# A two-layer cross-attention on one core: loads on two queues, a reordered front, and the statistics and normals of the main loop moved behind the maximum

## The chip, the cores and the metric

The kernel runs on one core of one Trainium2 chip. The metric is the device time in microseconds (us) of one execution. The core has five engines that matter here, each with its own instruction stream in program order: TensorE (PE, matrix multiplications and transposes), VectorE (DVE), ScalarE (ACT), GpSimd (POOL) and SyncE (SP, which here only issues loads and stores). They meet only through counted semaphores: an instruction waits until a count is reached, and all that stands behind it on its engine waits with it.

## The reference

The input is 32 batches of 256 tokens by 256 features, `x` and `ctx`. Layer 0 is a 16-head attention whose result for batch 0 alone (`att[0]`) is added to every batch. Layer 1 normalises both sides, attends over the normalised context, passes the result through a hidden layer of 4, attends over that once more, and adds it up.

```
q, k, v = heads(tgt @ Wq.T), heads(memory @ Wk.T), heads(memory @ Wv.T)
att = softmax(q k^T / sqrt(16)) v
x = tgt + att[0]                                # layer 0

norm_X, norm_F_L = LN(ctx, w1, b1), LN(x, w2, b2)
attended = softmax(norm_F_L norm_X^T / 16) norm_X
h = gelu(attended @ fc1_w.T + fc1_b)
cross = h @ fc2_w.T + fc2_b
norm_cross = LN(cross, w3, b3)
self = softmax(norm_cross norm_cross^T / 16) norm_cross
out = norm_F_L + gamma2 * (cross + gamma1 * self)
```

## The kernel before

Every engine's program is written out by hand, and nothing reorders it: what stands first in the code is issued first. The work falls into four stages.

The **front** (to about 14 us) loads the parameters, the transposed batch 0 of both inputs and the three weights, all on SP's queue, and then the first 8 batches (`SLOTS`) of `ctx` and `x` into `cN` and `xN`. PE first multiplies a constant by itself (`keep_busy`), then makes Q (into `qT`), K and the parameter products (`operand_products`), and the two halves of V (`value_projection`). VectorE prepares small operands one after the other (`link`: each waits for the one ahead of it), among them the output operand `stR` (`output_operand`, lines 336 to 347), and masks K into `kTm`.

The **head loop** (to about 37 us) does batch 0's 16 heads in 8 pairs `p`: scores, maxima, exponentials, transposes, products with V. Beside it VectorE takes the statistics of the context's first six batches and at `p == 6` their variances; GpSimd takes one root for all three pairs of batches and normalises them.

Then comes the **change of stage** (to about 55 us): `tgt2` (that is `att[0]`) is made and added to the first batches, and the `x` side of the first batches is normalised.

The **main loop** has 32 slots, one per batch `b`, and each engine has its own loop over them. Batches go in pairs: pair `k` holds batches `2k` and `2k+1`. In slot `b` PE does, in this order: `turned(k+1, m)` with `m = b % 2` (line 897: in an even slot it transposes the context side of the next pair, in an odd slot the `x` side of the next pair; it waits for the normalised halves of both batches of the pair), `score(b)` (line 960), one or two small products that depend on `b % 4`, and `weights_turned(b-1)` (line 968). ACT empties the transposes out of the PSUM banks, and makes the exponentials. The scores of a pair use transposes of the slots ahead.

A batch's way to `turned` goes over three engines. GpSimd adds `tgt2` to the `x` side (`add`, line 621). VectorE takes statistics of both sides (`statistics`, line 369), and of each pair the negative mean and the variance (`variances`, lines 377 and 380). GpSimd takes the inverse root (`root`, line 628, which also waits for the variances) and normalises the context side (line 641); VectorE normalises the `x` side (`normal`, line 389). VectorE also takes the maximum of the scores (`maximum(b)`, line 512), which waits for `score(b)`.

GpSimd's slot `b` is `add(b+6)`, then in an even slot `root(k+2)`, then the context side's `normal(b+4)`. VectorE's slot, the lines that the change moves:

```
if k + 3 < PAIRS:
    statistics(b + 6, 0)
    statistics(b + 6, 1)
    if m == 1:
        variances(k + 3)
maximum(b)
...
if k + 2 < PAIRS:
    normal(b + 4)
```

In the slots 20 to 29 VectorE has the first half of the algebra on the hidden layer as well (`LATE`). The **tail** (from about 168 us) does the second attention over `cross` and stores the output.

## Time and profile before

| | |
|---|---|
| timed runs | 245.39, 248.79 and 255.70 us, median 248.79 |
| profiled execution | 244.72 us, of which the span from first to last instruction is 242.9 |
| busy share of the span | PE 88%, DVE 79%, ACT 62%, POOL 51% |
| chain that ended last | PE 55%, DVE 27%, issue 8%, ACT 6%, POOL 1% |
| mean granted clock of PE | 0.967 of full speed |

The busy shares are means over stages with different limits, so they do not say which engine bounds a stage. The chain of waits, followed back from the last instruction, passes over VectorE, PE and ACT in turn up to 55 us, runs on PE alone from 59 to 117 us, is mixed with VectorE up to 147 us, and is on PE again up to 164 us.

### The profile page before, as it was taken

How to read it: one execution, taken by the hardware profiler on the slowest of the kernel's cores; microseconds unless marked ns; L12 is line 12 of the kernel's file. 1: busy time of each engine (PE TensorE's matmuls, PEld its weight loads, DVE VectorE, ACT ScalarE, POOL GpSimd, SP SyncE). 2: the span in 40 equal slices, each digit the busy share in tenths (PEclk: the TensorE clock that was granted, in tenths of full speed). 3: DMA queues.
4: the chain of work that ended last, by engine and by line, in shares of the span. 5: the costliest groups of instructions: out<-in, count | busy, mean ns of one | idle time of the engine just before them, and what ended most of it. 6: DMA issues, size and time to landing. Idle time of an engine off the chain costs nothing.

```text
span 242.9 us, 4973 instructions
## 1 busy us (share of the span) xinstructions
PE 212.8 (88%) x1758; PEld 154.1 (63%) x1758; DVE 193.1 (79%) x376; ACT 151.3 (62%) x292; POOL 124.4 (51%) x184
## 2 busy tenths in 40 slices
PE   6989989677999999999999899999978569999850
PEld 6766647445878789687796777967646234444420
DVE  7888858899999987798799999933557966777773
ACT  2167866216778678676796977856695435676520
POOL 6000096776999999969788948400002621221340
PEclk9999999999999999999999999999999857999995
DMA  6990000253454415554154000000000022443468
GB/s 183 381 346 3 1 4 0 81 155 111 174 173 136 164 53 173 175 153 159 51 174 158 3 1 3 0 1 3 0 3 1 0 89 86 172 168 149 174 229 326
DMA packets 14713, 26.82 MB, mean 110 GB/s; under 512 B 1760, under 2 KB 1760, under 8 KB 14688
## 3 DMA queue, kind: packets, MB, share of 16 engines
q1 hardware_dynamic: 14688, 26.50, 31.4%
q8 instruction: 14, 0.23, 0.4%
q14 instruction: 11, 0.09, 0.1%
HBM read 18.11 MB, written 8.39 MB: 109 GB/s over the span
## 4 chain that ended last, share of the span: by engine, by line
PE 55%; DVE 27%; issue 8%; ACT 6%; POOL 1%; DVEq 0%; ACTq 0%; POOLq 0%
PE psum L960 15%; PE psum L897 7%; DVE bn L369 6%; DVE xN L389 5%; PE psum L968 5%; PE psum L852 5%; DVE nm L552 3%; PE psum L1074 3%; PE psum L998 2%; PE psum L910 2%; PE psum L980 2%; PE psum L925 2%; PE psum L938 2%; DVE nmax L512 2%; DVE Fall L567 1%
## 5 line engine op out<-in xcount | busy, mean ns | idle before, releaser
L960 PE MATMUL psum<-XT,Fall 128*128 128x256 f32 x256 | 60.9, 381 | 1.8 <-ACT Fall L742 1.8
L960 PEld LDWEIGHTS psum<-XT,Fall 128*128 128x128 f32 x256 | 46.1, 190 | 7.2 <-ACT Fall L742 2.2
L641 POOL TENSOR_SCALAR cN<-cN,nmean,rstd 128x256 f32<-128x256 f32 x64 | 38.5, 612 | 2.4 <-POOL rstd L628 2.3
L621 POOL TENSOR_TENSOR xN<-xN,tgt 128x512 f32<-128x512 f32 x28 | 35.7, 1277 | 1.6 <-DVE xN L389 1.6
L389 DVE TENSOR_SCALAR xN<-xN,bn,rstd 128x256 f32<-128x256 f32 x64 | 34.1, 576 | 0.7 <-POOL rstd L628 0.7
L765 ACT ACTIVATE PT<-psum 128x512 f32<-128x512 f32 x32 | 19.1, 598 | 24.3 <-PE psum L968 24.2
L772 ACT ACTIVATE E<-psum,nmax 128x256 f32<-128x256 f32 x64 | 26.7, 474 | 11.0 <-DVE nmax L512 10.9
L628 POOL TENSOR_TENSOR rstd<-vps,minus_half 128x8 f32<-128x8 f32 (+1 forms) x16 | 25.0, 1564 | 15.7 <-DVE vps L380 15.6
L685 POOL CAST sC<-co 128x160 bf16<-128x160 f32 x8 | 2.6, 321 | 59.3 <-DVE co L561 59.3
L512 DVE TENSOR_REDUCE nmax<-psum 128x2 f32<-128x512 f32 x32 | 21.9, 685 | 13.8 <-PE psum L960 13.3
L567 DVE TENSOR_TENSOR Fall<-psum,Fall 128x1024 f32<-128x1024 f32 x15 | 18.1, 1219 | 10.1 <-PE psum L1107 10.1
L739 ACT ACTIVATE XT<-psum,b1s,w1s 128x512 f32<-128x512 f32 x32 | 23.1, 792 | 3.7 <-PE psum L897 3.7
L742 ACT ACTIVATE Fall<-psum,par 128x512 f32<-128x512 f32 x32 | 23.4, 796 | 3.2 <-PE psum L897 3.2
L852 PE MATMUL psum<-ident 128*128 128x128 f32 x144 | 23.3, 307 | 1.9 <-POOL ident L593 1.9
L852 PEld LDWEIGHTS psum<-ident 128*128 128x128 f32 x144 | 19.4, 208 | 5.5 <-issue 3.6
L369 DVE BATCH_NORM_STATS2 bn<-cN 128x6 f32<-128x512 f32 x32 | 22.3, 696 | 0.4 <-DVE r L445 0.2
L552 DVE TENSOR_REDUCE nm<-psum 128x4 bf16<-128x1024 f32 x16 | 19.5, 1218 | 3.4 <-PE psum L1042 3.3
L369 DVE BATCH_NORM_STATS2 bn<-xN 128x6 f32<-128x512 f32 x32 | 21.8, 687 | 0.0
L968 PE MATMUL psum<-ident,E 128*128 128x128 f32 x128 | 20.2, 280 | 0.3 <-ACT E L772 0.2
L968 PEld LDWEIGHTS psum<-ident,E 128*128 128x128 f32 x128 | 14.3, 141 | 8.3 <-issue 6.3
L897 PE MATMUL psum<-ident,xN 128*128 128x128 f32 x128 | 17.1, 274 | 2.6 <-DVE xN L389 2.3
L897 PE MATMUL psum<-ident,cN 128*128 128x128 f32 x128 | 16.9, 274 | 0.1
(157 smaller groups left out, 346.0 us busy)
## 6 DMA issues: line engine op xcount, KB each, us to landing
cN<-ctx SPq DMA_DIRECT2D x32, 256.0 KB, 2.9
xN<-x SPq DMA_DIRECT2D x32, 256.0 KB, 3.8
out<-Fall SPq DMA_DIRECT2D x32, 256.0 KB, 2.3
x0T<-x0t SPq DMA_DIRECT2D x1, 256.0 KB, 2.7
wqT<-wqt SPq DMA_DIRECT2D x1, 256.0 KB, 2.9
c0T<-c0t SPq DMA_DIRECT2D x1, 256.0 KB, 4.0
wkT<-wkt SPq DMA_DIRECT2D x1, 256.0 KB, 4.3
wvT<-wvt SPq DMA_DIRECT2D x1, 256.0 KB, 4.5
```

The lines of the kernel that those rows point to most:

```text
L369: dve.bn_stats(bn[:, (b // 2) % 4, side, b % 2, :], src[:, b % SLOTS, :].rearrange("p (t d) -> p d t", t=NT)).then_inc(st_ok, 1)
L389: dve.tensor_scalar(own, own, stat(p, 1, m, t, 1), root_of(p, 1, m, t), ALU.subtract, ALU.mult)\
L512: dve.tensor_reduce(nmax[:, b % 2, :], tiles(bank[SBANK1[b % 3]]), AX.X, ALU.max, negate=True)\
L552: dve.tensor_reduce(nm2[:, p % 2, :, 0:NT], scored(p).rearrange("p (m t k) -> p m t k", m=2, t=NT), AX.X, ALU.max, negate=True).then_inc(m ...
L621: pool.tensor_tensor(xN[:, b % SLOTS, :], xN[:, b % SLOTS, :], tgt2[:, :, :].rearrange("p t d -> p (t d)"), ALU.add).then_inc(y_ok, 1)
L628: pool.tensor_tensor(rstd[:, p % 4, sides, :].rearrange("p s k -> p (s k)"), vps[:, p % 4, sides, :].rearrange("p s k -> p (s k)"), minus_ ...
L641: pool.tensor_scalar(own, own, nmean[:, p % 4, NT * m + t:NT * m + t + 1], root_of(p, 0, m, t), ALU.add, ALU.mult)\
L772: act.activation(E[:, b % 2, t * N:(t + 1) * N], bank[SBANK1[b % 3]][:, t * N:(t + 1) * N], ACT.Exp, bias=nmax[:, b % 2, t:t + 1]).then_in ...
L852: pe.matmul(bank[b][:, 0:P], ident[:, :], ident[:, :], start=True, stop=True)
L897: last = pe.transpose(bank[TBANK[n % 3]][:, m * N + t * P:m * N + (t + 1) * P], z[:, (2 * p + m) % SLOTS, t * D + c * P:t * D + (c + 1) * ...
L960: last = pe.matmul(bank[SBANK1[b % 3]][:, t * N:(t + 1) * N], Fall[:, b, c, t * P:(t + 1) * P], XT[:, p % 4, c, m * N:(m + 1) * N], start= ...
L968: last = pe.transpose(bank[SBANK1[b % 3]][:, k * N + t * P:k * N + (t + 1) * P], E[:, b % 2, t * N + k * P:t * N + (k + 1) * P], ident[:, :])
```

## The change

It reorders the front and the main loop, and computes the same.

- **Loads.** `x0T` and `c0T` are issued by ACT's queue and the three weights by SP's, side by side. Behind them SP loads eight batches of `ctx` first and then eight of `x`.
- **Front on PE.** `keep_busy` multiplies `meanw`, which is GpSimd's first memset, eight times in place of seven. K is made and masked in two halves. The first half of V comes behind the first head scores and the second in the head loop's pass 2, and ACT copies them out in passes 1 and 3. `operand_products`, the first `project` and `project_back` move to the change of stage.
- **Output operand** on GpSimd, 17 small steps, each behind the one ahead.
- **Roots by pair.** The variances of the first three pairs are taken in the head loop's passes 1, 3 and 5, and GpSimd roots and normalises one pair at a time.
- **GpSimd's `add(5)`** waits until VectorE has normalised the first four batches of `x`.
- **Main loop on VectorE.** In slot `b` the maximum now comes first, then the statistics of batch `b+5` (in place of `b+6`), in an even slot the variances of the pair of `b+5`, and last the normal of batch `b+3` (in place of `b+4`). PE's, ACT's and GpSimd's slots keep their order.

```diff
-        for dst, src, arrived in ((x0T, x0t, q_in), (wqT, wqt, q_in), (c0T, c0t, k_in), (wkT, wkt, k_in),
-                                  (wvT, wvt, v_in)):
-            sp.dma_start(dst[:, :, :], src).then_inc(arrived, 16)
-
-        for p in range(PAIRS):
-            if p >= SLOTS // 2:
-                sp.wait_ge(t_mm, turns_to(p - SLOTS // 2, 1))
+        sp.dma_start(wqT[:, :, :], wqt).then_inc(q_in, 16)
+        sp.dma_start(wkT[:, :, :], wkt).then_inc(k_in, 16)
+        sp.dma_start(wvT[:, :, :], wvt).then_inc(v_in, 16)
+
+        for src, dst, arrived in ((c_d, cN, c_in), (x_d, xN, x_in)):
+            for b in range(SLOTS):
+                sp.dma_start(dst[:, b, :], src[b, :, :]).then_inc(arrived[b], 16)
+        for p in range(SLOTS // 2, PAIRS):
+            sp.wait_ge(t_mm, turns_to(p - SLOTS // 2, 1))
...
-        def output_operand(part):
-
-            if part == 0:
...
-        output_operand(0)
-        dve.wait_ge(k_mm, 1)
-        for e, m in enumerate(("even", "odd")):
-            dve.tensor_scalar(kTm[:, e, :, :], tiles(bank[1]), c_(m), None, ALU.mult).then_inc(kT_ok, 1)
-        dve.wait_ge(qk_mm, 1)
-        link(dve.tensor_copy(Q[:, :], bank[5][:, 0:(H + 1) ** 2]))
-        link(dve.tensor_copy(K[:, :], bank[5][:, 64:64 + U * U]), "QK")
-        output_operand(1)
+        def masked(o):
+            dve.wait_ge(k_mm, o + 1)
+            for e, m in enumerate(("even", "odd")):
+                dve.tensor_scalar(kTm[:, e, o, :], bank[(1, 5)[o]][:, 0:N], c_(m), None, ALU.mult).then_inc(kT_ok, 1)
+
+        masked(0)
...
+        def first_variances(p):
+            dve.wait_ge(st_ok, 2 * p + 2)
+            dve.tensor_scalar(nmean[:, p, :].rearrange("p (m t) -> p m t", t=NT),
+                              bn[:, p, 0, :, :].rearrange("p m (t k) -> p m t k", t=NT)[:, :, :, 1],
+                              -1.0, None, ALU.mult).then_inc(vps_first, 1)
+            dve.tensor_scalar(vps[:, p, 0, :].rearrange("p (m t) -> p m t", t=NT),
+                              bn[:, p, 0, :, :].rearrange("p m (t k) -> p m t k", t=NT)[:, :, :, 2],
+                              1.0 / D, EPS, ALU.mult, ALU.add).then_inc(vps_first, 1)
...
+                if p == 0:
+                    masked(1)
                 if p < 2 * EARLY:
                     statistics(p, 0)
-                elif p == 2 * EARLY:
-                    dve.wait_ge(st_ok, 2 * EARLY)
-                    dve.tensor_scalar(nmean[:, 0:EARLY, :].rearrange("p q (m t) -> p q m t", t=NT),
-                                      bn[:, 0:EARLY, 0, :, :].rearrange("p q m (t k) -> p q m t k", t=NT)[:, :, :, :, 1],
-                                      -1.0, None, ALU.mult).then_inc(vps_first, 1)
-                    dve.tensor_scalar(vps[:, 0:EARLY, 0, :].rearrange("p q (m t) -> p q m t", t=NT),
-                                      bn[:, 0:EARLY, 0, :, :].rearrange("p q m (t k) -> p q m t k", t=NT)[:, :, :, :, 2],
-                                      1.0 / D, EPS, ALU.mult, ALU.add).then_inc(vps_first, 1)
+                if p in (1, 3, 5):
+                    first_variances(p // 2)
...
         add(3)
+        dve.wait_ge(qk_mm, 1)
+        link(dve.tensor_copy(Q[:, :], bank[7][:, 0:(H + 1) ** 2]))
+        link(dve.tensor_copy(K[:, :], bank[7][:, 64:64 + U * U]), "QK")
         normal(0)
         normal(1)
         statistics(2, 1)
...
         statistics(4, 1)
         normal(2)
         normal(3)
-        statistics(5, 1)
-        variances(2)
...
         for b in range(B):
             k, m, q = b // 2, b % 2, b // 4
-            if k + 3 < PAIRS:
-                statistics(b + 6, 0)
-                statistics(b + 6, 1)
-                if m == 1:
-                    variances(k + 3)
             maximum(b)
             if b % 4 == 2:
                 values(q)
             if b % 4 == 3 and q >= 1:
                 saved(q - 1)
-            if k + 2 < PAIRS:
-                normal(b + 4)
-            if b == 18:
-                output_operand(2)
+            if b == 0:
+                statistics(2 * EARLY - 1, 1)
+                variances(EARLY - 1)
+            elif b + 5 < B:
+                statistics(b + 5, 0)
+                statistics(b + 5, 1)
+                if m == 0:
+                    variances((b + 5) // 2)
+            if 4 <= b + 3 < B:
+                normal(b + 3)
             for part in LATE.get(b, ()):
                 algebra(0, part)
...
+        pool.memset(meanw[:, :], 1.0 / D).then_inc(consts, 1)
...
+        oc = [0]
+
+        def step(ins):
+            ins.then_inc(operand_ok, 1)
+            oc[0] += 1
+            pool.wait_ge(operand_ok, oc[0])
...
+        pool.wait_ge(alg, ALG["prods"])
+        step(pool.tensor_tensor(g12[:, :], c_("g1"), c_("g2"), ALU.mult))
+        for c in range(DC):
+            step(pool.tensor_scalar(Rt[:, c, 0:H], a5[:, c, 0:H], c_("g2", c), None, ALU.mult))
+            step(pool.tensor_scalar(Rt[:, c, H:CO], MT[:, c, :], g12[:, c:c + 1], None, ALU.mult))
+            step(pool.tensor_scalar(Rcut[:, c, 0:1], a5[:, c, H:H + 1], c_("g2", c), None, ALU.mult))
+            step(pool.tensor_tensor(Rt[:, c, CO - 1:CO], Rt[:, c, CO - 1:CO], Rcut[:, c, 0:1], ALU.add))
+        for part in range(2):
+            to = stR[:, :, part, :]
+            step(pool.tensor_copy(slots(to, CO, SLOTS_L[0]), repeated(Rt[:, :, :], 3)))
+            step(pool.tensor_tensor(Rcut[:, :, :], Rt[:, :, :], to[:, :, 0:CO], ALU.subtract))
+            step(pool.tensor_copy(slots(to, CO, SLOTS_L[1]), repeated(Rcut[:, :, :], 2)))
+            step(pool.tensor_tensor(to[:, :, 5 * CO:6 * CO], Rcut[:, :, :], to[:, :, 3 * CO:4 * CO], ALU.subtract))
+        ALG["stR"] = oc[0]
...
+            if b == 5:
+                pool.wait_ge(zy_ok, 8)
...
-        pool.wait_ge(vps_first, 2)
-        pool.tensor_tensor(rstd[:, 0:EARLY, 0, :], vps[:, 0:EARLY, 0, :],
-                           minus_half[:, 0:EARLY * 2 * NT].rearrange("p (q k) -> p q k", q=EARLY), ALU.pow)\
-            .then_inc(root_first, 1)
-        for b in range(2 * EARLY):
-            normal(b)
+        for p in range(EARLY):
+            pool.wait_ge(vps_first, 2 * p + 2)
+            pool.tensor_tensor(rstd[:, p, 0, :], vps[:, p, 0, :], minus_half[:, 0:2 * NT], ALU.pow).then_inc(root_first, 1)
+            normal(2 * p)
+            normal(2 * p + 1)
...
+        act.dma_start(x0T[:, :, :], x0t).then_inc(q_in, 16)
+        act.dma_start(c0T[:, :, :], c0t).then_inc(k_in, 16)
...
+            if p in (1, 3):
+                values_copied(p // 2)
...
+        turned_values(0)
...
-            if b % 4 == 1:
+            if b % 4 == 1 and q >= 1:
...
-                pe.matmul(bank[b][:, 0:P], ident[:, :], ident[:, :], start=True, stop=True)
-
-        pe.wait_ge(consts, 4)
-        keep_busy(7, 4)
+                pe.matmul(bank[b][:, 0:P], meanw[:, :], meanw[:, :], start=True, stop=True)
+
+        pe.wait_ge(consts, 1)
+        keep_busy(8, 4)
...
+        pe.wait_ge(k_in, 32)
+        for o in range(2):
+            for c in range(DC):
+                last = pe.matmul(bank[(1, 5)[o]][:, 0:N], wkT[:, c, o * P:(o + 1) * P], c0T[:, c, :],
+                                 start=c == 0, stop=c == DC - 1)
+            last.then_inc(k_mm, 1)
...
-        operand_products()
-        pe.wait_ge(v_in, 16)
-        value_projection(0)
...
-                if p == 1:
-                    pe.wait_ge(v1_ok, 2)
...
+                pe.wait_ge(v_in, 16)
+                value_projection(0)
+            if p == 2:
                 value_projection(1)
             if 1 <= p <= NHP:
                 if p == 1:
-                    pe.wait_ge(alg, ALG["QK"])
+                    pe.wait_ge(kT_ok, 4)
...
-        keep_busy(11, 7)
...
+        project(0)
+        operand_products()
+        keep_busy(3, 0)
+        project_back(0)
+        keep_busy(4, 0)
...
-            if b % 4 == 1 and q < QUADS:
+            if b % 4 == 1 and 1 <= q < QUADS:
                 project(q)
             if b % 4 == 2:
-                project_back(q)
+                if q >= 1:
+                    project_back(q)
```

VectorE in the main loop, slot 2 and the first of slot 3, before: `nmax` is the maximum, `V1` the values' copy of slot 2, `xN` the normals, `BN_STATS` the statistics.

```order
L369 BN_STATS bn<-cN 128x6
L369 BN_STATS bn<-xN 128x6
L512 TENSOR_REDUCE nmax<-psum 128x2
L523 COPY V1<-psum 128x8x4
L389 TENSOR_SCALAR xN<-xN,bn,rstd 128x256 x2
L369 BN_STATS bn<-cN 128x6
L369 BN_STATS bn<-xN 128x6
L377 TENSOR_SCALAR nmean<-bn 128x4
L380 TENSOR_SCALAR vps<-bn 128x8
L512 TENSOR_REDUCE nmax<-psum 128x2
```

And now:

```order
L505 TENSOR_REDUCE nmax<-psum 128x2
L516 COPY V1<-psum 128x8x4
L356 BN_STATS bn<-cN 128x6
L356 BN_STATS bn<-xN 128x6
L364 TENSOR_SCALAR nmean<-bn 128x4
L367 TENSOR_SCALAR vps<-bn 128x8
L376 TENSOR_SCALAR xN<-xN,bn,rstd 128x256 x2
L505 TENSOR_REDUCE nmax<-psum 128x2
```

The normals stood right behind a slot's maximum, and the statistics and variances between them and the next maximum; now statistics and variances follow the maximum and the normals come last.

VectorE ahead of the main loop's first maximum, before, from the normals of batches 2 and 3:

```order
L389 TENSOR_SCALAR xN<-xN,bn,rstd 128x256 x4
L369 BN_STATS bn<-xN 128x6
L380 TENSOR_SCALAR vps<-bn 128x4
L369 BN_STATS bn<-cN 128x6
L369 BN_STATS bn<-xN 128x6
L512 TENSOR_REDUCE nmax<-psum 128x2
L389 TENSOR_SCALAR xN<-xN,bn,rstd 128x256 x2
```

And now, from the same normals to the second maximum:

```order
L376 TENSOR_SCALAR xN<-xN,bn,rstd 128x256 x4
L505 TENSOR_REDUCE nmax<-psum 128x2
L356 BN_STATS bn<-xN 128x6
L367 TENSOR_SCALAR vps<-bn 128x4
L505 TENSOR_REDUCE nmax<-psum 128x2
L356 BN_STATS bn<-cN 128x6
L356 BN_STATS bn<-xN 128x6
L376 TENSOR_SCALAR xN<-xN,bn,rstd 128x256 x2
```

Between the normals and the first maximum stood four instructions, of which three are statistics; now the maximum follows the normals at once.

## Rows read from the trace of the kernel before

**Rows 1.** The windows view: length, busy us of PE, PEld, DVE, ACT, POOL, clock, DMA.

```profile
5.40:15.00 9.60, 8.99 (x52) 6.99 (x52) 7.66 (x28) 2.70 (x7) 0.00 (x0) 1.00 1.03 383
37.40:59.40 22.00, 16.56 (x116) 12.52 (x115) 20.79 (x42) 9.34 (x16) 14.67 (x16) 1.00 0.30 96
59.40:117.00 57.60, 57.56 (x442) 47.22 (x441) 50.74 (x103) 44.06 (x87) 53.20 (x58) 1.00 0.44 147
189.00:195.00 6.00, 2.85 (x30) 1.54 (x29) 5.86 (x8) 2.60 (x5) 4.18 (x8) 0.82 0.00 0
195.00:200.00 5.00, 3.18 (x24) 1.63 (x26) 3.41 (x6) 1.83 (x3) 1.46 (x4) 0.50 0.29 108
```

**Rows 2.** The timeline of PE, four slots: start, length, instruction.

```profile
93.26 1.89 PE L960 MATMUL psum<-XT,Fall 128*128 128x256 f32 x8
...
96.30 1.89 PE L960 MATMUL psum<-XT,Fall 128*128 128x256 f32 x8
...
100.47 1.89 PE L960 MATMUL psum<-XT,Fall 128*128 128x256 f32 x8
...
103.98 1.04 PE L897 MATMUL psum<-ident,xN 128*128 128x128 f32 x8
104.85 1.89 PE L960 MATMUL psum<-XT,Fall 128*128 128x256 f32 x8
...
108.11 1.89 PE L960 MATMUL psum<-XT,Fall 128*128 128x256 f32 x8
```

**Rows 3.** The timeline of VectorE in slots 14 and 15.

```profile
102.40 0.69 DVE L512 TENSOR_REDUCE nmax<-psum 128x2 f32<-128x512 f32 x1 [1.61 <-PE psum L960]
103.00 0.18 DVE L523 COPY V<-psum 128x32 f32<-128x32 f32 x1
...
104.78 0.69 DVE L369 BATCH_NORM_STATS2 bn<-cN 128x6 f32<-128x512 f32 x1
...
106.11 0.17 DVE L377 TENSOR_SCALAR nmean<-bn 128x4 f32<-128x4 f32 x1
106.19 0.16 DVE L380 TENSOR_SCALAR vps<-bn 128x8 f32<-128x8 f32 x1
```

**Rows 4.** The timeline of all engines: one root, two normals on each side.

```profile
77.23 0.16 DVE L380 TENSOR_SCALAR vps<-bn 128x8 f32<-128x8 f32 x1
...
77.47 1.65 POOL L628 TENSOR_TENSOR rstd<-vps,minus_half 128x8 f32<-128x8 f32 x1 [0.18 <-DVE vps L380]
...
78.01 0.72 DVE L389 TENSOR_SCALAR xN<-xN,bn,rstd 128x256 f32<-128x256 f32 x2
...
79.29 1.09 POOL L641 TENSOR_SCALAR cN<-cN,nmean,rstd 128x256 f32<-128x256 f32 x2 [0.18 <-POOL rstd L628]
80.34 1.27 POOL L621 TENSOR_TENSOR xN<-xN,tgt 128x512 f32<-128x512 f32 x1
81.60 1.29 POOL L641 TENSOR_SCALAR cN<-cN,nmean,rstd 128x256 f32<-128x256 f32 x2
```

**Rows 5.** The timeline of VectorE ahead of and at the loop's start.

```profile
43.55 1.38 DVE L389 TENSOR_SCALAR xN<-xN,bn,rstd 128x256 f32<-128x256 f32 x4 [0.31 <-POOL rstd L628]
...
47.54 3.27 DVE L389 TENSOR_SCALAR xN<-xN,bn,rstd 128x256 f32<-128x256 f32 x4 [0.43 <-POOL rstd L628]
...
52.75 0.67 DVE L512 TENSOR_REDUCE nmax<-psum 128x2 f32<-128x512 f32 x1
```

**Rows 6.** The timeline of PE: scores of slot 2 and of slot 28.

```profile
55.69 1.99 PE L960 MATMUL psum<-XT,Fall 128*128 128x256 f32 x8 [0.66 <-ACT Fall L742]
...
154.30 1.89 PE L960 MATMUL psum<-XT,Fall 128*128 128x256 f32 x8
```

**Rows 7.** The chain of waits, head of the program: start, length, line.

```profile
1.90 3.36 PE psum L852 x14
...
9.16 0.81 PE psum L874 x8
...
13.71 1.16 PE psum L910 x8
```

More of the change, by code:

```diff
@@ L53 @@
 QUADS = B // 4
+EARLY = 3
 SLOT = 64
@@ L634, in normal @@
             if p < EARLY:
[L635 removed]
+                pool.wait_ge(root_first, p + 1)
             else:
@@ L861, in _ @@
         last.then_inc(mean_mm, 1)
-        for arrived, n, w, src, b, done in ((q_in, 32, wqT, x0T, 0, q_mm), (k_in, 32, wkT, c0T, 1, k_mm)):
-            pe.wait_ge(arrived, n)
-            for o in range(2):
-                for c in range(DC):
-                    last = pe.matmul(bank[b][:, o * N:(o + 1) * N], w[:, c, o * P:(o + 1) * P], src[:, c, :],
-                                     start=c == 0, stop=c == DC - 1)
-            last.then_inc(done, 1)
+        pe.wait_ge(q_in, 32)
+        for o in range(2):
+            for c in range(DC):
+                last = pe.matmul(bank[0][:, o * N:(o + 1) * N], wqT[:, c, o * P:(o + 1) * P], x0T[:, c, :],
+                                 start=c == 0, stop=c == DC - 1)
+        last.then_inc(q_mm, 1)
+        pe.wait_ge(k_in, 32)
+        for o in range(2):
+            for c in range(DC):
+                last = pe.matmul(bank[(1, 5)[o]][:, 0:N], wkT[:, c, o * P:(o + 1) * P], c0T[:, c, :],
+                                 start=c == 0, stop=c == DC - 1)
+            last.then_inc(k_mm, 1)
         def operand_products():
```

36 lines of the change are left out of this document (15 added, 21 removed).

## The prediction

> **What bounds the kernel now.** I read the chain of waits first, for where it stays on one engine: from 59 to 117 us it is PE alone. The windows view confirms it: PE is busy for 57.56 of 57.60 us there, GpSimd for 53.20, VectorE for 50.74 [rows 1]. So whatever makes PE wait in the main loop adds to the time one for one, while work taken from VectorE gives nothing. Ahead of the loop it is otherwise: from 37.4 to 59.4 PE is busy for 16.56 of 22.00 us and VectorE for 20.79, so there VectorE's order is what counts.
>
> The timeline of PE shows what the loop costs [rows 2]. Slot 12's scores start at 93.26, slot 13's at 96.30, slot 14's at 100.47, slot 15's at 104.85, slot 16's at 108.11: 14.85 us for four slots, without a gap. The transposes ahead of a score take 0.87 (103.98 to 104.85).
>
> **The main loop, step by step.** Let e be an even slot. In slot e+1 PE transposes the x side of batches e+2 and e+3. Before, the normal of batch e+3 stood on VectorE right behind the maximum of slot e-1, so it was done before PE wanted it. Now it stands in slot e, behind that slot's maximum, two statistics and the variances, and this maximum waits for score(e). PE's program is in order, so score(e+1) stands behind transposes that wait for a result of score(e): a loop over two engines where there was none.
>
> Its length, from the start of score(e): the maximum starts 1.93 later (100.47 to 102.40) and holds VectorE for 0.60; where slot e is the third of four, the values' copy adds 0.10 [rows 2, 3]. The two statistics up to the negative mean take 1.33, the mean 0.08, the variance 0.16 [rows 3], the two normals 0.72, as where they ran beside a root [rows 4]. That is 4.82, or 4.92. Two of the pair's eight transposes do not need batch e+3; the other six take 0.65. So score(e+1) starts 5.47 or 5.57 after score(e), where it took 3.04 (slot 12 to 13) and 4.38 (slot 14 to 15): PE's small work between fills only part of the wait.
>
> A second loop goes over GpSimd. The variances of the pair of batches e+4 and e+5 are now taken in slot e behind the maximum, where they used to be taken ahead of the maximum of slot e-1. GpSimd then does the root, a normal, an add and a normal, and PE's slot e+2 transposes these batches. From score(e): 1.93 + 0.60 + 1.33 + 0.08 as above; 0.24 to the root, 1.82 to the first normal, 1.05 to the add, 1.26 to the second normal, and 1.29 of that [rows 4]; 0.65 of transposes. That is 10.25, and 10.35 with the values' copy. PE's own way, with the first loop, is 5.47 + 4.17 = 9.64, or 5.57 + 3.26 = 8.83 [rows 2]. The longer sets the pair: about 10.3 where two slots now take 7.43. Both loops close anew in every pair, so slack ahead of the loop does not help.
>
> Thirteen pairs lie between the scores of slot 2 and of slot 28: six at 10.25, six at 10.35, and the last without its add (10.35 - 1.26 = 9.09), 132.7 us. Before it was 154.30 - 55.69 = 98.6 [rows 6]. That is **+34.1**. Slot 29 waits for one more normal, without statistics: 1.93 + 0.60 + 0.72 + 0.65 = 3.90 in place of 3.04, **+0.9**. VectorE's algebra in the slots from 20 on now lies behind the normals and beside PE's transposes and scores; it costs nothing as long as it fits into the wait that the second loop leaves VectorE. Its eight operand steps, now on GpSimd, lay beside a busy PE: nothing. On GpSimd the 17 steps lie where it did nothing at all (0.00 us busy from 5.4 to 15 us [rows 1]) and ahead of a first root that needs them no earlier; cover gone, each would cost a fraction of a us once.
>
> **The change of stage and the front.** Four normals took 3.27 beside GpSimd's adds and 1.38 alone [rows 5]; `add(5)` now waits for them, which gives 1.89. The first maximum came at 52.75, 1.94 behind the end of those normals, and now follows at once. Together 3.83 for the first exponentials, and with them for the evacuation and score(2) behind them on ACT. But the adds that waited now run beside the normals of batch 4, half as many: about 0.95 back, and 0.15 for the copies of the parameter products. I take 2.7. Bounds: 1.5, if the late adds hold up the slots' statistics as well, and 3.8.
>
> In the head the parameter products' 0.81 leave PE's path, and the second head score no longer waits for V (it started at 13.71) [rows 7]. K's halves let the first score start before the second half is masked. That is worth up to 2.4 at the second score; V's second half in pass 2, on PE about as long as a head score's 1.16, the copies on ACT and the small variances on VectorE take part of it back. I take 1.3, bounds 0 and 2.4. PE's warm-up starts earlier, behind the first memset, but has eight products in place of seven, and 3.36/7 = 0.48 of that is lost again [rows 7]; this is inside the bounds. Front in all **-4.0** (-1.5 to -6.2).
>
> Of the two load queues I expect nothing that can be seen: PE is busy for 8.99 of 9.60 us from 5.4 to 15, so at most 0.6 is waited for there, and the DMA engines are full (share 1.03) [rows 1]. The Trainium skill (Trainium Kernel Development and Optimization, Key Constraints) says that DMAs from SP's and ACT's queues run on the same 16 engines, and that several issuers save issue time alone. The full share agrees; by the rule the term is zero, against it 0.6 at most.
>
> Sum: 242.9 + 34.1 + 0.9 - 4.0 = 273.9 of span. Around the span lie 244.72 - 242.9 = 1.8: 275.7 against the profiled execution. The median of the timed runs lies 4.1 above that execution and the lowest 0.7; I add 2.3, between them: **278.0**.
>
> **Rivals.**
>
> *GpSimd is not the longer loop (0.11).* If its normals come without the add between them mattering, only the first loop holds: 6 x 9.64 + 7 x 8.83 = 119.7, +21.0 in place of +34.1, and 265. For it: GpSimd has more free time in a slower loop; against it: root, normal, add and normal are in order, and the lengths above are those of single instructions.
>
> *PE's clock falls (0.12).* In the first loop PE would stand still for some 2.4 us once in four slots (4.82, less the 3.04 - 0.87 of score and weights and the 0.22 of the first two transposes [rows 2]). The clock was at full speed where PE was busy for 75% (37.4 to 59.4), and fell to half after a stretch with 2.85 of 6.00 busy [rows 1]; the new loop has 7.43 of 10.3, 72%. At half speed the second loop grows by a score and the transposes, 1.89 + 0.65, to 12.8, and PE's own way, 9.24 on average, by 1.89 + 0.65 + 3.7 to 15.5. If it is half for half of the time, 13 pairs take 13 x 12.9 = 168: 35 us more, 313.
>
> *The shift is absorbed (0.08).* The other side: if normal(e+3) is ready within 2.17 + 0.22 = 2.4 us of score(e)'s start, where PE's own work ends, PE sees no wait, and the front's gain stands alone: 242.9 - 4.0 + 1.8 + 2.3 = 243. The rows give 4.82, so VectorE's part would have to take less than half of its time. I leave it a chance only for an error in my reading of who waits for whom: 0.04 faster, 0.04 within 2%.
>
> *Root and normals exclude each other (0.03).* If the normals could not start before the root ends (0.24 + 1.65 behind the variance's start instead of 0.16), score(e+1) would start 1.7 later, pairs take 11.4 and 10.6, and 13 of them 142: 287. But two normals took 0.72 in the middle of a root of 1.65 [rows 4]. The Trainium skill (SBUF, Who interferes with whom) says that VectorE's `tensor_scalar` in its two-port mode and any GpSimd instruction hold one shared pair of ports in turn, and that the later one waits for the whole of the other. The 3.27 beside the adds agrees with it; the 0.72 beside the root does not, and that is the neighbour that the normals of even slots will have.
>
> **How the numbers follow.** The forecast is the likeliest case, 278 (0.66). Its own spread: instructions beside GpSimd's that come 0.5 later in each pair (+6.5), a front that gives 1.5 (+2.5), the median's place (-1.6 to +1.8), and a clock that falls now and then. The range goes from 262, below the first rival, to 296; it leaves out the clock at half for long and the absorbed shift, 0.20 together. A change within 2% is about what cannot be told from none here. Slower by over 2%: all but the absorbed case, 0.92.
>
> **What would show it.** In the changed kernel's main loop PE has gaps in every pair: one ahead of the x side's transposes, released by VectorE's normals, and one ahead of the context side's, released by GpSimd's. VectorE's maximum starts at once behind the score, and VectorE and GpSimd stand idle in every pair too. Score 2 starts near 51.7, and score 28 some 133 us later. The first maximum follows its normals at once. I am wrong if PE stays busy without gaps from 59 to 117, if the gaps are there but only VectorE ends them, or if the granted clock in the loop is below 1.

## The result and the profile after

The changed kernel takes **278.23 us** (median of 4 runs, 275.83 to 278.85) against 250.51 for the kernel before (4 runs, 245.39 to 255.7). The ratio is 1.124, with an interval of 1.107 to 1.142: slower. The profiled execution took 278.69 us, 276.9 of it span. Ratios leave out executions in which a lower granted clock had lengthened the whole run.

The windows view of the changed kernel first. Its columns are the window, its length, then the busy us of PE, PEld, DVE, ACT and POOL, the granted clock, the DMA share and GB/s.

```profile
5.40:15.00 9.60, 9.29 (x54) 6.84 (x54) 6.97 (x20) 3.53 (x9) 4.21 (x17) 1.00 1.04 389
...
59.00:117.00 58.00, 45.94 (x321) 35.74 (x323) 33.97 (x70) 31.56 (x61) 35.63 (x40) 0.96 0.35 109
117.00:185.00 68.00, 52.09 (x392) 39.95 (x384) 48.20 (x108) 40.49 (x75) 40.76 (x46) 1.00 0.20 63
```

In the main loop PE is busy for 45.94 of 58.00 us, where it had been for 57.56 of 57.60 [rows 1]. No engine is full: VectorE has 33.97 and GpSimd 35.63. A loop in which all engines wait is bound by a chain that goes from one to the next. The waits view of the loop from 72 to 182 us names its links (sum in us, times, longest):

```profile
POOL rstd L648 <- DVE vps L367: 43.8, 11, 5.1
DVE nmax L505 <- PE psum L993: 36.8, 20, 4.4
...
PE psum L930 <- DVE xN L376: 17.5, 11, 2.3
...
PE psum L930 <- POOL cN L661: 8.3, 10, 1.3
```

GpSimd waits for the variances, VectorE for the scores, and PE once in a pair for VectorE's normals and once for GpSimd's. One pair of it, in the timeline of all engines (start, length, engine, line, instruction; the wait ahead of it in brackets):

```profile
104.55 1.89 PE L993 MATMUL psum<-XT,Fall 128*128 128x256 f32 x8
...
106.48 0.69 DVE L505 TENSOR_REDUCE nmax<-psum 128x2 f32<-128x512 f32 x1 [0.99 <-PE psum L993]
...
107.09 0.69 DVE L356 BATCH_NORM_STATS2 bn<-cN 128x6 f32<-128x512 f32 x1
...
108.49 0.16 DVE L367 TENSOR_SCALAR vps<-bn 128x8 f32<-128x8 f32 x1
108.56 0.73 DVE L376 TENSOR_SCALAR xN<-xN,bn,rstd 128x256 f32<-128x256 f32 x2
108.73 1.74 POOL L648 TENSOR_TENSOR rstd<-vps,minus_half 128x8 f32<-128x8 f32 x1 [3.71 <-DVE vps L367]
109.35 0.87 PE L930 MATMUL psum<-ident,xN 128*128 128x128 f32 x6 [2.25 <-DVE xN L376]
...
110.06 1.89 PE L993 MATMUL psum<-XT,Fall 128*128 128x256 f32 x8
...
110.65 1.09 POOL L661 TENSOR_SCALAR cN<-cN,nmean,rstd 128x256 f32<-128x256 f32 x2 [0.18 <-POOL rstd L648]
...
111.70 1.27 POOL L641 TENSOR_TENSOR xN<-xN,tgt 128x512 f32<-128x512 f32 x1
...
112.96 1.09 POOL L661 TENSOR_SCALAR cN<-cN,nmean,rstd 128x256 f32<-128x256 f32 x2
...
113.81 1.68 DVE L376 TENSOR_SCALAR xN<-xN,bn,rstd 128x256 f32<-128x256 f32 x2
...
114.10 0.87 PE L930 MATMUL psum<-ident,cN 128*128 128x128 f32 x6 [0.37 <-POOL cN L661]
...
114.81 1.89 PE L993 MATMUL psum<-XT,Fall 128*128 128x256 f32 x8
```

Read down it goes round once: score of slot 12, maximum 1.93 later, two statistics, the variance, the root, GpSimd's normal, add and normal, the transposes, and the score of slot 14. 104.55 to 114.81 is 10.26 us, where slots 12 and 13 had needed 7.21 (93.26 to 100.47 [rows 2]). The x side's loop closes inside it: 104.55 to 110.06, 5.51.

PE's timeline at the loop's start answers to [rows 6], VectorE's to [rows 5]. PE:

```profile
50.48 1.99 PE L993 MATMUL psum<-XT,Fall 128*128 128x256 f32 x8
...
58.01 3.02 PE L993 MATMUL psum<-XT,Fall 128*128 128x256 f32 x8
...
62.20 1.89 PE L993 MATMUL psum<-XT,Fall 128*128 128x256 f32 x8
...
67.00 1.49 PE L930 MATMUL psum<-ident,xN 128*128 128x128 f32 x6 [2.25 <-DVE xN L376]
68.28 3.00 PE L993 MATMUL psum<-XT,Fall 128*128 128x256 f32 x8
...
186.01 1.89 PE L993 MATMUL psum<-XT,Fall 128*128 128x256 f32 x8
```

VectorE:

```profile
46.07 1.38 DVE L376 TENSOR_SCALAR xN<-xN,bn,rstd 128x256 f32<-128x256 f32 x4 [0.43 <-POOL rstd L648]
47.53 0.69 DVE L505 TENSOR_REDUCE nmax<-psum 128x2 f32<-128x512 f32 x1
...
51.97 1.91 DVE L376 TENSOR_SCALAR xN<-xN,bn,rstd 128x256 f32<-128x256 f32 x2
53.80 0.68 DVE L505 TENSOR_REDUCE nmax<-psum 128x2 f32<-128x512 f32 x1
```

Score 2 starts at 50.48 (before 55.69), score 28 at 186.01 (before 154.30): the 13 pairs take 135.53 in place of 98.61. Two scores, of slots 3 and 5, take 3.02 and 3.00 in place of 1.89, at a clock that had fallen (0.59 of full speed from 57.0 to 61.0 and from 67.0 to 71.2). From score 31 (197.30) to the end it is 79.6; before, 164.55 to 242.9, 78.4.

### The profile page after: what moved, and what is told of

Read it like the earlier page. It is cut to its first block and busy times, and to the rows that moved or that the text cites. A ratio compares the mean times of both kernels' runs of the same rounds, so it can differ in the third digit from the quotient of the medians.

```text
span 276.9 us, 4969 instructions
## 1 busy us (share of the span) xinstructions
PE 222.0 (80%) x1752; PEld 157.3 (57%) x1752; DVE 185.9 (67%) x367; ACT 153.2 (55%) x292; POOL 125.6 (45%) x203
## 5 line engine op out<-in xcount | busy, mean ns | idle before, releaser
L993 PE MATMUL psum<-XT,Fall 128*128 128x256 f32 x256 | 63.1, 391 | 1.1 <-ACT Fall L767 1.1
L648 POOL TENSOR_TENSOR rstd<-vps,minus_half 128x8 f32<-128x8 f32 (+1 forms) x16 | 26.1, 1628 | 60.4 <-DVE vps L367 60.1
L993 PEld LDWEIGHTS psum<-XT,Fall 128*128 128x128 f32 x256 | 47.9, 198 | 7.1 <-ACT Fall L767 1.5
L930 PE MATMUL psum<-ident,xN 128*128 128x128 f32 x128 | 21.0, 292 | 24.0 <-DVE xN L376 24.0
L661 POOL TENSOR_SCALAR cN<-cN,nmean,rstd 128x256 f32<-128x256 f32 x64 | 34.8, 554 | 2.6 <-POOL rstd L648 2.3
L376 DVE TENSOR_SCALAR xN<-xN,bn,rstd 128x256 f32<-128x256 f32 x64 | 34.1, 578 | 0.5 <-POOL rstd L648 0.4
L930 PEld LDWEIGHTS psum<-ident,xN 128*128 128x128 f32 x128 | 15.1, 147 | 27.7 <-DVE xN L376 26.2
L930 PE MATMUL psum<-ident,cN 128*128 128x128 f32 x128 | 19.3, 279 | 8.3 <-POOL cN L661 8.3
L878 PE MATMUL psum<-meanw 128*128 128x128 f32 x138 | 23.3, 314 | 1.0 <-POOL meanw L583 1.0
L878 PEld LDWEIGHTS psum<-meanw 128*128 128x128 f32 x138 | 19.2, 212 | 4.6 <-issue 3.6
L930 PEld LDWEIGHTS psum<-ident,cN 128*128 128x128 f32 x128 | 14.1, 141 | 11.7 <-POOL cN L661 10.9
```

The lines of the kernel that those rows point to most:

```text
L376: dve.tensor_scalar(own, own, stat(p, 1, m, t, 1), root_of(p, 1, m, t), ALU.subtract, ALU.mult)\
L648: pool.tensor_tensor(rstd[:, p % 4, sides, :].rearrange("p s k -> p (s k)"), vps[:, p % 4, sides, :].rearrange("p s k -> p (s k)"), minus_ ...
L661: pool.tensor_scalar(own, own, nmean[:, p % 4, NT * m + t:NT * m + t + 1], root_of(p, 0, m, t), ALU.add, ALU.mult)\
L878: pe.matmul(bank[b][:, 0:P], meanw[:, :], meanw[:, :], start=True, stop=True)
L930: last = pe.transpose(bank[TBANK[n % 3]][:, m * N + t * P:m * N + (t + 1) * P], z[:, (2 * p + m) % SLOTS, t * D + c * P:t * D + (c + 1) * ...
L993: last = pe.matmul(bank[SBANK1[b % 3]][:, t * N:(t + 1) * N], Fall[:, b, c, t * P:(t + 1) * P], XT[:, p % 4, c, m * N:(m + 1) * N], start= ...
```

## The experiments

The places that every run below is read by, from its profiled execution: the start of score 2, the 13 pairs from there to score 28, and what lies between score 31 and the end of the span. The median is of all timed runs; the ratio leaves out the same executions as above.

| kernel | span | clock | score 2 | 13 pairs | after score 31 | median | ratio (interval) |
|---|---|---|---|---|---|---|---|
| before | 242.9 | 0.967 | 55.69 | 98.6 | 78.4 | 246.3 to 250.5 | |
| after | 276.9 | 0.954 | 50.48 | 135.5 | 79.6 | 278.23 | 1.124 (1.107 to 1.142) |
| e1_slots_back | 243.2 | 0.949 | 54.62 | 98.5 | 79.9 | 244.20 | 0.997 (0.994 to 0.9996) |
| e2_slots_only | 280.5 | 0.945 | 55.83 | 135.3 | 78.1 | 281.74 | 1.146 (1.138 to 1.154) |
| e3_normals_first | 295.1 | 0.923 | 49.99 | 154.1 | 79.8 | 298.66 | 1.215 (1.203 to 1.226) |
| e4_variances_early | 277.2 | 0.920 | 49.82 | 138.1 | 77.9 | 279.08 | 1.136 (1.131 to 1.142) |
| e6_first_max | 245.7 | 0.944 | 50.79 | 103.1 | 81.6 | 249.56 | 1.004 (0.9997 to 1.008) |
| e5_first_max_busy | 249.0 | 0.923 | 50.49 | 103.0 | 85.2 | 251.24 | 1.021 (1.014 to 1.028) |
| e7_adds_together | 280.4 | 0.913 | 50.77 | 138.5 | 79.8 | 282.15, one run | |
| e8_busy_3_5 | 275.5 | 0.957 | 50.63 | 135.6 | 78.0 | 277.32, one run | |
| e9_adds_busy | 279.8 | 0.906 | 50.37 | 128.7 | 88.9 | 281.62 and 269.88 | |
| e10_after_busy | 277.2 | 0.955 | 50.88 | 134.7 | 79.8 | 279.52 | 1.136 (1.127 to 1.145) |
| e11_tail_busy | 239.9 | 0.973 | 53.94 | 99.7 | 76.1 | 242.35 | 0.986 (0.981 to 0.992) |
| e12_before_tail | 242.6 | 0.979 | 56.40 | 98.6 | 77.4 | 244.13 | 0.995 (0.992 to 0.998) |

**Which part of the change costs the time?** e1 takes VectorE's main loop back and keeps the rest; e2 makes that edit alone in the kernel before.

```diff
 e1, against the changed kernel (e2 is the same edit the other way, in the kernel before)
+        statistics(5, 1)
+        variances(2)
         for b in range(B):
+            if k + 3 < PAIRS:
+                statistics(b + 6, 0)
+                statistics(b + 6, 1)
+                if m == 1:
+                    variances(k + 3)
             maximum(b)
...
-            if b == 0:
-                statistics(2 * EARLY - 1, 1)
-                variances(EARLY - 1)
-            elif b + 5 < B:
-                statistics(b + 5, 0)
-                statistics(b + 5, 1)
-                if m == 0:
-                    variances((b + 5) // 2)
-            if 4 <= b + 3 < B:
-                normal(b + 3)
+            if k + 2 < PAIRS:
+                normal(b + 4)
```

> The changed kernel with VectorE's main loop alone put back: statistics of batch b+6 and the variances ahead of maximum(b), normal(b+4) behind it, and statistics(5, 1) and variances(2) ahead of the loop. Theory (the two loops through score, maximum and normals make all of the loss): PE has no gaps from slot 4 on, the scores of slot 2 and slot 28 lie 98 to 100 us apart again instead of 135.5 (186.01 - 50.48), and the front keeps most of its gain, so the span is 239 to 242 against 276.9 now and 242.9 before. Rival (the front is what slows: operand steps on GpSimd, the add(5) that waits for zy_ok 8, loads in another order): most of the loss stays, a span over 265.

> The kernel before with VectorE's main loop of the changed one, nothing else. Theory: the whole loss comes back, the scores of slot 2 and slot 28 lie 132 to 137 us apart, pairs take 10.25 and 10.35, and without the front's gain of head and add(5) the span is 277 to 281. Rival (the front is part of the loss): a span under 265.

The two runs split the change in two without a rest. With the slots put back the pairs take 98.5 again, with the slots alone 135.3. The whole loss lies in the order of VectorE's slot. What e1 does not keep is most of the front's gain: score 2 comes 1.1 earlier than before, not 4 to 5, and 0.3% is left of it at the end. That part of its expectation missed: the span is 243.2, not 239 to 242.

**Is it the loop that was named?** e3 and e4 each shift one link of the chain, so that the two theories of its length part.

```diff
 e3, against the changed kernel
             if b % 4 == 3 and q >= 1:
                 saved(q - 1)
+            if 4 <= b + 3 < B:
+                normal(b + 3)
...
-            if 4 <= b + 3 < B:
-                normal(b + 3)
```

> The changed kernel, with normal(b+3) right behind the slot's maximum and the statistics and variances behind it. This shortens the loop over VectorE from 5.47 to 1.93 + 0.60 + 0.72 + 0.65 = 3.90 and lengthens the way to the variances by the two normals, 0.65 to 0.72. Theory (the longer loop over GpSimd sets the pair, 10.26 and 10.36 in the trace): pairs get LONGER, to 10.9 to 11.1, and 13 pairs take 8 to 9 us more than the changed kernel's; the gap ahead of the x side's transposes nearly goes (to under 1 us) and the one ahead of the context side's grows by about 2. Rival (VectorE's late normals are what costs, GpSimd is slack that follows): pairs fall to 7.9 to 8.1, 13 pairs to some 103, the span to about 246.

With VectorE's normals ahead of the statistics PE's first pause should shrink, and the way to the root should grow. It did both. The timeline of all engines of e3, over the end of one pair and the next:

```profile
90.36 0.88 PE L930 MATMUL psum<-ident,xN 128*128 128x128 f32 x6 [0.53 <-DVE xN L376]
...
97.28 0.87 PE L930 MATMUL psum<-ident,cN 128*128 128x128 f32 x6 [1.80 <-POOL cN L661]
```

VectorE's normals now end only 0.53 of PE's pauses here, and GpSimd's 1.80. Pairs without a fallen clock took 10.95 to 10.98 (63.66 to 74.62, 74.62 to 85.60, 108.97 to 119.92), as the loop over GpSimd said; had VectorE's normals been the bound, they would have come down. Thirteen such pairs would be 142.5, near the 143.5 to 144.5 expected. The other 11.6 of the 154.1 lie in the first pair (13.67) and in pairs with a score at a fallen clock: those of slots 8, 14, 18 and 26 took 3.33 to 3.52 (granted clock 0.54 from 85.6 to 89.0). No run held the clock in e3.

```diff
 e4, against the changed kernel
-            elif b + 5 < B:
-                statistics(b + 5, 0)
-                statistics(b + 5, 1)
-                if m == 0:
-                    variances((b + 5) // 2)
+            if b + 6 < B:
+                statistics(b + 6, 0)
+                statistics(b + 6, 1)
+                if m == 1:
+                    variances((b + 6) // 2)
```

> The changed kernel, with the statistics one batch further ahead (b+6) behind the maximum, and the variances of a pair in the odd slot ahead, as early as in the kernel before; normal(b+3) stays last. This takes the loop over GpSimd away and leaves the one over VectorE without variances: 1.93 + 0.60 + 1.24 + 0.72 + 0.65 = 5.14, 5.24 with the values' copy. Theory: no gap that GpSimd ends; pairs take 5.14 + 4.17 = 9.31 and 5.24 + 3.26 = 8.50, 13 pairs 115 us, the span about 256 to 259. Rival (the normals' place alone is the loss, so nothing is won): 13 pairs stay at 130 or more.

The variances move into the odd slot, so the root is early. The loop over GpSimd opens indeed: no pause of PE in the loop is ended by GpSimd any more, and the pairs that begin in the third of four slots take 8.76 (95.76 to 104.52; 8.50 expected). But those that begin in the first of four take 12.06 (83.70 to 95.76; 9.31 expected). The timeline there:

```profile
87.44 1.70 DVE L376 TENSOR_SCALAR xN<-xN,bn,rstd 128x256 f32<-128x256 f32 x2
87.70 1.29 POOL L641 TENSOR_TENSOR xN<-xN,tgt 128x512 f32<-128x512 f32 x1
...
89.20 1.23 PE L930 MATMUL psum<-ident,xN 128*128 128x128 f32 x6 [2.96 <-DVE xN L376]
...
90.22 3.26 PE L993 MATMUL psum<-XT,Fall 128*128 128x256 f32 x8
```

The early root has pushed GpSimd's add beside VectorE's normals, which now take 1.70 in place of 0.73. PE's pause grows to 2.96, the clock falls (0.59 from 89.2 to 93.4), and the score takes 3.26. The expectation missed: one loop went, the other grew by 1.0, and the clock fell behind the longer pause. Of the 2.75 over the 9.31 expected, the normals are 0.97, the slower transposes 0.36 (1.23 against 0.87) and the slower score 1.37. That the clock would have stood without the longer pause was not tried in e4. e7 tries the same from GpSimd's side, with both adds in the even slot, ahead of the root, so that nothing stands between its two normals.

```diff
 e7, against the changed kernel (GpSimd's slot)
-            if k + 3 < PAIRS:
+            if m == 0 and k + 3 < PAIRS:
                 add(b + 6)
+                add(b + 7)
```

> The changed kernel, with GpSimd's adds of both batches of a pair in the even slot, ahead of the root, so that no add lies between the two normals of a pair. Theory: the loop over GpSimd shrinks by 1.26, to 8.99 and 9.09, and the other loop takes over where it is longer: pairs of 9.64 (even slot the first of four) and 9.09 (third of four), 13 pairs 121 to 125 us instead of 135.5, the span near 265; the gap that GpSimd ends goes in the first kind of pair. Rival (GpSimd does not set the pair): no change of the distance of the scores.

Again GpSimd ends no pause, and again only every other pair is short: 9.15 (96.76 to 105.91; 9.09 expected), then 11.46 (105.91 to 117.37) in place of 9.64. PE's timeline in e7:

```profile
105.91 1.89 PE L994 MATMUL psum<-XT,Fall 128*128 128x256 f32 x8
...
110.86 0.88 PE L931 MATMUL psum<-ident,xN 128*128 128x128 f32 x6 [2.23 <-DVE xN L376]
111.58 3.19 PE L994 MATMUL psum<-XT,Fall 128*128 128x256 f32 x8
```

The pause is 2.23, no longer than the 2.25 of the changed kernel at 109.35, and score to score is 5.67 against its 5.51; but here the score takes 3.19 (granted clock 0.64 from 111.0 to 114.7), there 1.89. That asked for a run in which only the clock differs. e9 is e7 with seven filler products of TensorE in every fourth slot, which take up part of the pause; e10 is the changed kernel with the same filler.

```diff
 e9, against e7; e10, against the changed kernel (PE's slot)
+            if b % 4 == 1 and q >= 1 and k + 1 < PAIRS:
+                pe.wait_ge(V1_ok, q)
+                keep_busy(7, 6)
```

> e7 (both adds in one slot) with seven filler products of TensorE at the start of every fourth slot, behind the wait for the weighted values. Two theories of why e7's shorter pairs gave no shorter loop. If it was the granted clock, which fell to half at each of e7's scores behind the two adds (2.94 to 3.62 us in place of 1.89), the filler holds it: scores near 1.89, pairs of 9.64 and 9.15 in turn, some 122 us for the 13 pairs and a span near 265. If the pairs are long because VectorE's chain is long there and the clock only follows it, the scores shorten and the pause ahead of them grows by as much: pairs of 11.5 and 9.15 as in e7, a span of 279 to 281, or a little more for the filler itself.

The filler held the clock. The windows view from 72 to 188 us, of e9:

```profile
72.00:188.00 116.00, 104.27 (x803) 83.34 (x795) 83.09 (x177) 72.31 (x137) 71.23 (x82) 1.00 0.25 81
```

and of e7:

```profile
72.00:188.00 116.00, 97.44 (x663) 72.15 (x662) 72.47 (x165) 66.14 (x125) 68.36 (x78) 0.92 0.25 82
```

PE's timeline of e9, over one such pair:

```profile
102.04 1.89 PE L994 MATMUL psum<-XT,Fall 128*128 128x256 f32 x8
...
107.01 0.87 PE L931 MATMUL psum<-ident,xN 128*128 128x128 f32 x6 [0.85 <-DVE xN L376]
107.72 1.89 PE L994 MATMUL psum<-XT,Fall 128*128 128x256 f32 x8
...
111.88 1.89 PE L994 MATMUL psum<-XT,Fall 128*128 128x256 f32 x8
```

Score to score is 5.68 as in e7, so VectorE's chain is as long as it was, and the filler lay wholly in the pause. But the score takes 1.89, and the pair 9.84 (102.04 to 111.88) in place of 11.46, the other still 9.15. From slot 4 to slot 28 every score of e9 takes 1.89. The first theory holds for these pairs: it was the clock that ate e7's gain. The 13 pairs come to 128.7, not 122, mostly since slots 2 to 4 took 13.87: the filler starts with slot 5, and slot 3's score took 3.62. Behind the loop the granted clock was 0.80 from 190 to 240, and the last part took 88.9, so the span of 279.8 says little of the loop. The other timed run had a span of 268.0, near the 265 expected.

e8, ahead of these, had filler in slots 3 and 5 of the changed kernel alone.

```diff
 e8, against the changed kernel
+            if b in (3, 5):
+                keep_busy(7, 7)
```

> The changed kernel, with seven extra products on PE (results not used) at the start of the slots 3 and 5, in the two pauses behind which the clock fell to half and scores took 3.02 and 3.00. Theory (what is over the forecast in the loop is the clock): both scores take 1.89, the scores of slots 2 and 28 lie 133 us apart instead of 135.5, the granted clock is 1.00 up to 74 us. Rival (the pairs at the start are longer because GpSimd and VectorE run beside each other there): the distance stays within 0.5 of 135.5.

> The changed kernel with the same filler. The 13 pairs took 135.53 us against 132.7 forecast, and two long scores (3.02 and 3.00) stood in the excess. If these falls of the clock are the excess, and the filler takes them away: 132 to 134 for the 13 pairs, span 274 to 276. If the filler doesn't reach them (an earlier one at slots 3 and 5 only moved a fall to slot 9), 135.5 and a span of 276 to 277. Either way the loop's 10.25 to 10.36 a pair stays, since the filler lies on TensorE and the loop runs over VectorE and GpSimd.

e8 missed: slot 5's score took 1.89, but slot 3's still 3.16, and slot 9's 2.99 in its place; the 13 pairs stayed at 135.6. In e10 all scores from slot 4 to slot 29 take 1.89, and the 13 pairs 134.7, between its two cases: 12 of them 122.96 (62.63 to 185.59) against 122.45 by the prediction's lengths. Slots 4 to 6 took 10.29, in the changed kernel 11.36. Slots 2 to 4 stayed at 11.75. The span still came to 277.2, since score 2 came 0.4 later and the way from score 28 to the end took 0.7 more; 0.5 of that lies ahead of score 29 (4.61 in place of 4.08), where the filler takes 1.73 and the pause was 0.83.

**Where did the front's gain go?** e6 keeps before's order from slot 1 on, but lets the first maximum follow its normals; e5 adds filler in PE's slot 2, ahead of the transposes of slot 1's weights.

```diff
 e6, against e1; e5 has in PE's slot 2, beside that, keep_busy(8, 7)
-        statistics(5, 1)
-        variances(2)
...
-            if k + 3 < PAIRS:
+            if b > 0 and k + 3 < PAIRS:
                 statistics(b + 6, 0)
                 statistics(b + 6, 1)
...
             maximum(b)
+            if b == 0:
+                statistics(5, 1)
+                variances(2)
+                statistics(6, 0)
+                statistics(6, 1)
             if k + 2 < PAIRS:
                 normal(b + 4)
```

> The changed kernel with VectorE's main loop as in the kernel before, except in slot 0: there the maximum comes first, and behind it statistics(5, 1), variances(2), the statistics of batch 6 and normal(4). So the first maximum follows its normals as in the changed kernel, and from slot 1 on no normal waits for a score of the slot ahead. Theory: the front's gain is kept; slot 2's scores start near 50.5 instead of 55.69 and slot 4's near 60 instead of 63.47, the scores of slots 4 and 28 lie 91 us apart as in the kernel before, the span is 239 to 241 and the time 0.97 to 0.99 of before. Rival (the gain is spent again at the loop's start, since normals and statistics have to catch up there, as in the run with the loop put back): slot 4's scores start at 62 or later and the time is 0.99 to 1.00 of before.

> The same, and PE gets eight extra products (into a bank that nobody uses there, results not used) between score(2) and weights_turned(1), where it would stand still for VectorE. If the clock falls there without them, slot 3's scores take 1.9 instead of 3 to 3.6 and slot 4 starts about 1 us earlier than in the run without them; if the clock does not matter, slot 4 starts at the same time or up to 1 us later.

Score 2 comes at 50.79, as early as in the changed kernel, but slot 4's at 63.26, where it was 63.31 before (63.47 in expectations is the same start, as the chain of waits gives it): the 4.9 us of score 2 were spent within two slots, as the rival in its expectation had it. The windows view of e6:

```profile
52.00:56.00 4.00, 0.79 (x4) 0.36 (x2) 3.96 (x7) 0.00 (x0) 2.29 (x3) 1.00 0.37 138
56.00:63.20 7.20, 6.02 (x32) 5.58 (x33) 7.17 (x15) 4.23 (x9) 6.84 (x8) 0.76 0.30 98
```

and of the kernel before:

```profile
56.00:63.20 7.20, 6.20 (x42) 5.40 (x40) 7.13 (x16) 4.46 (x10) 6.06 (x7) 1.00 0.28 100
```

Two things spent it. First, VectorE is full (3.96 of 4.00) while PE does 0.79 of 4.00: the same statistics and normals stand ahead of the second maximum in whichever order. So PE's transposes of slot 1's weights start only 1.78 earlier than before. PE's timeline in e6:

```profile
57.18 0.86 PE L1003 MATMUL psum<-ident,E 128*128 128x128 f32 x4 [4.39 <-ACT E L799]
...
63.26 1.89 PE L995 MATMUL psum<-XT,Fall 128*128 128x256 f32 x8
```

and in the kernel before:

```profile
58.96 0.60 PE L968 MATMUL psum<-ident,E 128*128 128x128 f32 x4
...
63.31 1.89 PE L960 MATMUL psum<-XT,Fall 128*128 128x256 f32 x8
```

Second, from there to score 4 PE works without a pause in e6 and takes 6.08, where the same products took 4.35 before. The granted clock is 0.76 in that window of e6 and 1.00 in that of before, with VectorE full in both. So up to 1.7 of the 4.9 went to the clock.

e5 was to part the two and does not. Its filler left the clock low (0.51 from 56.8 to 59.4), and 6.05 pass from those transposes (56.89) to score 4. Slot 3's score took 2.29 in place of 2.58, and score 4 came 0.3 earlier (62.94), but score 2, ahead of the filler, had come 0.3 earlier already: 12.45 from score 2 to score 4 against 12.47. What e6's front would be worth at a held clock stays open. e5's last part came out longer, at a lower clock in the run as a whole.

**A version that beats both.** As in the kernel before [rows 1], the clock falls in e1's last part. e11 is e1 with more filler there; e12 has the same filler in the kernel before, to tell it from the front.

```diff
 e11, against e1; e12, against the kernel before
             if p == QUADS:
+                keep_busy(6, 4)
...
-                keep_busy(5 if p < 5 else 2, 5)
+                keep_busy(9 if p in (4, 5) else 5 if p < 5 else 2, 5)
```

> e1 (VectorE's slots put back, the rest of the change kept), with more filler products in the last slots, where the granted clock stood at half over some 8 us and TensorE paused 1.19 to 1.82 us. If the clock is what the tail loses: 1 to 3 us less than e1's 244.2, so 241.5 to 243.2, a ratio of 0.985 to 0.995 against the kernel before. If the tail is set by its chain of VectorE and GpSimd steps: the same as e1 (0.996), or up to 1 us more, since the filler itself stands ahead of products that are ready.

> The kernel before, with nothing of the change, and e11's filler in its last slots. e11 (the change without VectorE's new slots, with the filler) was measured at 242.35 us, e1 (without the filler) at 244.2. If the filler alone is e11's gain and the change's front is worth nothing that lasts to the end: 242 to 243, a ratio of 0.984 to 0.990, level with e11. If the front is worth the 1 to 1.5 us by which its score of slot 4 and of slot 28 came earlier than before (62.34 against 63.47, 153.09 against 154.30): 243 to 244.5, a ratio of 0.990 to 0.997, and e11 stands below it.

The same 8 us in the windows view of e1:

```profile
192.00:200.00 8.00, 4.67 (x33) 2.09 (x33) 5.14 (x9) 1.84 (x3) 1.79 (x5) 0.50 0.19 68
```

and of e11:

```profile
192.00:200.00 8.00, 7.08 (x74) 4.58 (x73) 5.96 (x11) 2.86 (x7) 2.30 (x6) 1.00 0.19 68
```

PE's timeline there shows that filler stands where pauses stood, in e1:

```profile
193.51 0.29 PE L1090 MATMUL psum<-identb,nm 128*64 128x128 bf16 x1 [1.52 <-DVE co L554]
...
196.16 0.59 PE L1064 MATMUL psum<-identb,sU 128*128 128x128 bf16 x4 [1.82 <-issue]
```

and in e11:

```profile
194.03 0.22 PE L1091 MATMUL psum<-identb,nm 128*64 128x128 bf16 x1 [0.38 <-DVE co L554]
...
196.64 0.40 PE L1065 MATMUL psum<-identb,sU 128*128 128x128 bf16 x4 [0.53 <-DVE sU L305]
```

e11 takes 242.35 us, 1.4% less than the kernel before; the last part of its profiled execution is 3.8 shorter than e1's, in part since e1's clock fell a second time (0.83 from 213.3 to 223.3), and the medians are 1.85 apart. The filler alone (e12) gives 244.13, 0.5% less. By these two medians the front is worth 1.8. At score 31 between 0.7 and 1.4 of it is seen: 163.84 in e11, 164.55 in the kernel before, and 165.22 in e12, whose code is the same up to there. So the second of e12's cases held, and the best kernel here is this change without its new order of VectorE's slot, with filler at the end.

## Why the prediction held

*What bounds the kernel and what goes wrong there* held: the new loops are there, the one over GpSimd is the longer, and both close in every pair. The loop's terms against the rows above: 1.93 to the maximum (forecast 1.93), 0.61 and 1.32 to the mean (0.60, 1.33), 0.08, then 2.16 to the first normal (0.24 + 1.82), 1.05, 1.26, 1.14 of the second (1.29), 0.71 of transposes (0.65): 10.26, where 10.25 was forecast; the pair ahead of it, with the values' copy, took 10.36 (94.19 to 104.55; 10.35). The first loop is 5.51 and 5.61 (94.19 to 99.80; 5.47 and 5.57). The last pair took 9.19 (9.09).

*+34.1* measured +36.9. The two first pairs make 2.5 of the difference. Slots 2 to 4 took 11.72: slot 2's maximum came 3.32 behind its score (53.80 less 50.48), not 1.93, since the normals of batch 4 ahead of it took 1.91 beside an add. The forecast had priced them, as 0.95 off the front's gain, and not in the loop, where they fell. Slots 4 to 6 took 11.36, since slot 5's score ran at a fallen clock; e10 took that fall away and got 10.29. The eleven others took 112.45 against 112.1.

*Slot 29* +0.9: measured 4.08 in place of 3.04, +1.0. The last part was not in the sum and took 1.2 more (79.6 against 78.4): the clock fell there a second time (0.84 from 257.0 to 267.5). It is no cost of the change, since e4 and e8, with the same code there, took 77.9 and 78.0.

*Front -4.0* measured -5.2 at score 2. The head gave 1.44 (24 context transposes at 36.06, before at 37.50) against 1.3, the change of stage 3.77 against 2.7; the first maximum follows its normals at once, as the step said, and they took 1.38, not 3.27. The 0.95 that was taken off here came back as the 1.39 of slot 2. What the step did not say is that this gain need not last: with the old order behind it (e6) it is gone by slot 4.

*Two load queues, 0*: PE was busy for 9.29 of the 9.60 us in question and the DMA share is 1.04, so no more than 0.3 is left to wait for. No run has the two queues alone.

*From the span to the median* the sum added 2.3, and the profiled execution lies 0.5 above its median. This error, 2.8, and the 3.0 by which the span was forecast too short cancel: that 278.0 was hit so closely is luck, the side and the mechanism are not.

*The rivals.* That GpSimd is not the longer loop fell with e3. That the shift is absorbed fell with the waits view. The clock at half for long fell in the changed kernel (1.00 from 117 to 185). But the third sign that the prediction gave for being wrong, a granted clock below 1 in the loop, did come: 0.96 from 59 to 117, from the two falls at slots 3 and 5 (it is 1.00 from 71.5 to 185), of which the second cost 1.1. And the rival lay one step away: e7's pairs lost 9.8 us to it (138.5 against e9's 128.7), and e3's up to 11.6 (154.05 against 13 of 10.96, the longer first pair included). That root and normals exclude each other fell at 108.56: two normals of 0.73 were done at 109.29, 1.18 ahead of the end of a root of 1.74 that began at 108.73. The Trainium skill (SBUF, Who interferes with whom) has VectorE's `tensor_scalar` in its two-port mode and any GpSimd instruction take turns at a shared pair of ports. Beside the adds the rows bear it out (1.68, 1.70, 1.91), beside the root they do not.

## What to carry to other kernels

Before moving a step behind another in an engine's order, follow what it feeds until the chain comes back to what it now waits for. If it comes back, add up the loop and compare it with the full engine's time: here 10.3 against 7.4 a pair, which no slack ahead of the loop can hide.

A gain at the head of a stage is followed to where it is to be kept: an engine that is full there, or a clock that falls in the new pauses, can spend it. e6's score 2 was 4.9 us earlier, and slot 4's 0.05.

Where a change makes the full engine pause, look at the granted clock beside each pause, and let one run hold the clock by filler, as e9 did: it tells a long chain from a slow clock. Check that the clock did hold; in e5 and, at slot 3, in e8 it did not.
